# An attention layer's products in column tiles in a projection bank, and the next scores ahead of the transposes

## The reference

```python
q = heads(hidden_states @ W_q)                       # 20 heads of 8
k_t, v_t = heads(text_ehs @ W_k), heads(text_ehs @ W_v)
probs_t = softmax(q k_t^T * attn_scale)              # 128 x 73 for a head
text_out = probs_t @ v_t
qsem = l2norm(probs_t @ text_ehs)                    # 128 x 256 for a head
sem = qsem @ l2norm(ip_ehs)^T                        # 128 x 4
probs_ip = softmax(q k_ip^T * attn_scale + 0.5 * sem) * spatial_mask
out = (text_out + probs_ip @ v_ip) @ W_out + b_out + residual
```

## Time and profile before

| | |
|---|---|
| median of 3 runs | 3484.98 us (3480.99 to 3485.95) |
| profiled execution | 3485.28 us, span 3483.4 us |
| TensorE granted clock, mean | 0.99 |
| busy PE, DVE, ACT, POOL | 96%, 70%, 66%, 38% |
| DMA | 313.84 MB, mean 90 GB/s |

### The profile page before, as it was taken

How to read it: one execution, slowest core, us unless ns; L and a number is a source line. 1 busy time by engine, 2 the same in 40 slices (tenths; PEclk the granted TensorE clock), 3 DMA queues, 4 the chain that set the end, 5 groups by cost and what they waited for, 6 DMA issues and landing times. The chain is left out here.

```text
span 3483.4 us, 96098 instructions
## 1 busy us (share of the span) xinstructions
PE 3335.4 (96%) x34878; PEld 3131.8 (90%) x34878; DVE 2438.3 (70%) x7677; ACT 2314.2 (66%) x6485; POOL 1329.5 (38%) x1657
## 2 busy tenths in 40 slices
PE   5899999999999999999999999999999999999997
PEld 4789999999899999999999899998999999899987
DVE  6657677767767767677767767767677776777655
ACT  4566676766767676676766767676676766767654
POOL 2223343333434433343433434433343333434333
PEclk9999999999999999999999999999999999999998
DMA  6432324223142332324223142332324223142310
GB/s 157 157 116 69 105 63 126 74 86 103 54 123 70 108 90 68 108 63 122 78 83 105 54 123 68 106 94 63 113 64 118 82 82 106 54 124 68 94 51 11
DMA packets 210732, 313.84 MB, mean 90 GB/s; under 512 B 31232, under 2 KB 167520, under 8 KB 210272
## 3 DMA queue, kind: packets, MB, share of 16 engines
q1 hardware_dynamic: 209984, 307.53, 30.5%
q10 hardware_dynamic: 288, 0.16, 0.0%
HBM read 267.97 MB, written 14.42 MB: 81 GB/s over the span
## 5 line engine op out<-in xcount | busy, mean ns | idle before, releaser
L997 ACT ACTIVATE SE<-PS,mx 128x77 f32<-128x77 f32 (+1 forms) x2560 | 674.8, 355 | 271.9 <-DVE mx L1248 271.2
L1461 POOL TENSOR_TENSOR SE<-SE,rs 128x512 f32<-128x512 f32 (+1 forms) x640 | 552.7, 869 | 625.7 <-DVE rs L1270 625.7
L1454 POOL TENSOR_TENSOR n<-qq,p_half 128x4 f32<-128x4 f32 x320 | 327.4, 1023 | 987.0 <-DVE qq L1299 987.0
L1265 DVE TENSOR_REDUCE sums<-SE 128x4 f32<-128x512 f32 (+1 forms) x640 | 368.3, 576 | 217.8 <-ACT SE L997 217.3
L985 ACT ACTIVATE PTs<-PT 128x1024 f32<-128x1024 f32 (+1 forms) x320 | 326.5, 1020 | 242.3 <-PE PT L811 240.7
L933 ACT ACTIVATE qk<-PG 128x512 f32<-128x512 f32 (+1 forms) x640 | 326.3, 510 | 127.2 <-PE PG L612 125.5
L773 PE MATMUL PW<-w_o,OTs 128*128 128x160 f32 x2560 | 408.8, 303 | 0.0
L1248 DVE TENSOR_REDUCE mx<-PS 128x8 f32<-128x1024 f32 (+1 forms) x320 | 323.0, 1010 | 115.6 <-PE PS L793 113.4
L827 PE MATMUL PV<-PTs,v_sb 128*64 128x128 f32 (+1 forms) x5120 | 351.1, 279 | 12.3 <-DVE SE L1291 12.0
L773 PEld LDWEIGHTS PW<-w_o,OTs 128*128 128x128 f32 x2560 | 359.7, 191 | 0.0
L876 PE MATMUL PV<-later 73*128 73x86 f32 x2560 | 331.0, 272 | 2.3 <-ACT later L1006 1.4
(11 more groups left out here) (209 smaller groups left out, 8439.1 us busy)
## 6 DMA issues: line engine op xcount, KB each, us to landing
q_slice<-q_split SPq DMA_DIRECT2D x630, 192.0 KB, 2.4
vc_slice<-vc_split SPq DMA_DIRECT2D x155, 512.0 KB, 4.0
kc_slice<-kc_split SPq DMA_DIRECT2D x150, 256.0 KB, 2.9
q1st<-q_hi SPq DMA_DIRECT2D x320, 32.0 KB, 2.1
k1st<-k_hi SPq DMA_DIRECT2D x160, 38.5 KB, 2.2
xres<-in_x_dram SPq DMA_DIRECT2D x32, 160.0 KB, 2.7
q1st<-q_lo SPq DMA_DIRECT2D x160, 32.0 KB, 2.1
out_dram<-x SPq DMA_DIRECT2D x64, 80.0 KB, 1.6
```

Source lines behind the costliest of these rows:

```text
L997: last = a_(SE[:, n % 4, J * i:J * i + J], PS[:, e, J * at:J * at + J], ACT.Exp, bias=mx[:, q % 2, 4 * e + at:4 * e + at + 1])
L1265: v.tensor_reduce(sums[:, n % 2, :], SE[:, n % 4, 0:4 * J].rearrange("p (i j) -> p i j", j=J), AX, ALU.add)\
L1454: gp.tensor_tensor(n20[:, b % 2, 4 * w:4 * w + 4], qq[:, b % 2, 4 * w:4 * w + 4], p_half[:, 0:4], ALU.pow)\
L1461: gp.tensor_tensor(e, e, rs[:, n % 2, :].unsqueeze(2).to_broadcast([128, 4, J]), ALU.mult)\
```

## The change

1. `probs_v1`'s product becomes a job: it is the first job of slot 0 of the beat after the one it was in, takes a PG bank instead of PV, and stands directly behind `probs_v`. Each of the four matmuls becomes two, with 64 weight columns each, to partitions 0 to 63 and 64 to 127 of the bank (column tiles).
2. `unit_out` moves along, to slot 0 behind `softmax_in`; `unit_norms` and `norms_of` move from slot 0 to slot 1. `tail_slot` grows by one and the tail's jobs shrink by one, so that jobs keep their slots and the VectorE parts are one slot later.
3. At the head of a beat `scores` of the next duo comes before `probs_transposed`.
4. Units of the last group (`alone`) have their scores in turn in PS and PT's second bank, ahead of the transposes of the unit before.

Semaphore `pv1_done` goes; `job_full` stands for it. `probs_v` no longer waits for `on_done`.

```diff
@@ -69,7 +69,7 @@
...
 CTX1_SLOT = {0: 65, 1: 80, 2: 95, 3: 110}
-TAIL_JOB = {"ipT": 7, "ip": 10, "oT1": 13, "y": 16}
+TAIL_JOB = {"ipT": 6, "ip": 9, "oT1": 12, "y": 15}
@@ -349,7 +349,13 @@
...
 def tail_slot(g, b):
-    return 3 * l1_beat(g, W1 * b + W1 - 1) + 7
+    return 3 * l1_beat(g, W1 * b + W1 - 1) + 8
+
+def alone(g, k):
+    return l1_beat(g, k) > DUOS * GROUPS + 1
+
+def scores1_bank(g, k):
+    return PS[:, 0, :] if alone(g, k) and k % 2 else PT[:, 1, :]
...
 def slots(at):
@@ -402,10 +408,12 @@
...
 def jobs_at(t):
...
+    unit = l1_at(t // 3 - 2) if t % 3 == 0 else None
+    products1 = [("pv1",) + unit] if unit else []
...
     first, v = first[:1], v + first[1:]
-    return first + v, [x for x in late_at(t) if x[0] != "v"]
+    return products1 + first + v, [x for x in late_at(t) if x[0] != "v"]
@@ -460,7 +468,7 @@
...
             "down": "down_added", "q1": "q1_done", "k1": "k1_done", "vip": "vip_done",
-            "ctx1": "gv_done", "ipT": "ipT_done", "ip": "o1_done", "oT1": "o1T_done", "y": "y_done"}
+            "ctx1": "gv_done", "pv1": "on_done", "ipT": "ipT_done", "ip": "o1_done", "oT1": "o1T_done", "y": "y_done"}
...
 def bank(name):
@@ -483,7 +491,7 @@
 def wait_gv_used(engine, g, b):
...
     if g0 >= 0:
-        engine.wait_ge(S["pv1_done"], l1_count(g0, W1 * b0 + W1 - 1))
+        engine.wait_ge(S["job_full"], JOB[("pv1", g0, W1 * b0 + W1 - 1)] + 1)
...
 def _(sp):
@@ -818,8 +826,6 @@
...
             pe.wait_ge(S["ots_done"], q)
-        if product1[0]:
-            pe.wait_ge(S["on_done"], product1[0])
@@ -829,7 +835,7 @@
...
-    scored1, turned1, product1 = [0], [0], [0]
+    scored1, turned1 = [0], [0]
...
     def scores1(g, k, turned):
@@ -837,12 +843,15 @@
...
             pe.wait_ge(S["pts_done"], turned)
-        if j > 1:
+        if alone(g, k - 1):
+            pe.wait_ge(S["exp1_done"], j - 2)
+            pe.wait_ge(S["exp_done"], NL0 * GROUPS)
+        elif j > 1:
...
         pe.wait_ge(S["kbd_done"], j)
-        mm(PT[:, 1, 0:4 * T], q1st[:, h, w, 128 * (b % HB):128 * (b % HB) + 128],
+        mm(scores1_bank(g, k)[:, 0:4 * T], q1st[:, h, w, 128 * (b % HB):128 * (b % HB) + 128],
@@ -860,44 +869,47 @@
...
-    def probs_v1(g, k, multiplied):
-
+    def probs_v1(g, k):
+
+        name = ("pv1", g, k)
         b, w, j = k // W1, k % W1, l1_count(g, k)
+        pe.wait_ge(*read_out(JOBS[JOB[name] - len(PG)]))
         pe.wait_ge(S["pts1_done"], j)
-        if multiplied:
-            pe.wait_ge(S["ots_done"], multiplied)
-        if j > 1:
-            pe.wait_ge(S["on_done"], j - 1)
...
             off = D1 * (i % 2)
-            last = mm(PV[:, GV * i + off:GV * i + off + GS + D1], PTs1[0:TT, 128 * i:128 * i + 128],
-                      gv[:, b % 2, 2 * w + i // 2, off:off + GS + D1], start=True, stop=True)
-        last.then_inc(S["pv1_done"], 1)
-        product1[0] = j
+            for c in range(2):
+                last = mm(bank(name)[64 * c:64 * c + 64, GV * i + off:GV * i + off + GS + D1],
+                          PTs1[0:TT, 128 * i + 64 * c:128 * i + 64 * c + 64],
+                          gv[:, b % 2, 2 * w + i // 2, off:off + GS + D1], start=True, stop=True)
+        last.then_inc(S["job_full"], 1)
...
         beat, part = divmod(t, 3)
-        turned, multiplied = min(max(beat + 1, 0), DUOS * GROUPS), min(max(beat, 0), DUOS * GROUPS)
+        turned = min(max(beat + 1, 0), DUOS * GROUPS)
         if part == 0:
+            if duo_at(beat + 1):
+                scores(*duo_at(beat + 1))
...
                 probs_transposed(*duo_at(beat))
-            if duo_at(beat + 1):
-                scores(*duo_at(beat + 1))
...
                 probs_v(*duo_at(beat - 1))
+            if l1_at(beat - 2):
+                probs_v1(*l1_at(beat - 2))
+        ahead = part == 1 and l1_at(beat) and alone(*l1_at(beat))
+        if ahead:
+            scores1(*l1_at(beat), turned)
...
             probs_transposed1(*l1_at(beat - 1), turned)
-        if part == 1 and l1_at(beat):
+        if part == 1 and l1_at(beat) and not ahead:
...
         for name in jobs_at(t)[0]:
-            job(name)
+            if name[0] != "pv1":
+                job(name)
...
             keep_busy(6)
-        if part == 2 and l1_at(beat - 1):
-            probs_v1(*l1_at(beat - 1), multiplied)
@@ -1002,7 +1014,7 @@
...
         if j > 1:
-            act.wait_ge(S["pv1_done"], j - 1)
+            act.wait_ge(S["job_full"], JOB[("pv1",) + divmod(j - 2, GB * W1)] + 1)
...
     def exp1(g, k):
@@ -1012,7 +1024,7 @@
...
         for i in range(4):
-            last = a_(SE1[:, j % 2, TT * i:TT * i + TT], PT[:, 1, T * i:T * i + TT], ACT.Exp,
+            last = a_(SE1[:, j % 2, TT * i:TT * i + TT], scores1_bank(g, k)[:, T * i:T * i + TT], ACT.Exp,
@@ -1253,7 +1265,7 @@
...
         dve.wait_ge(S["s1_done"], j)
-        sc = PT[:, 1, 0:4 * T].rearrange("p (i j) -> p i j", j=T)
+        sc = scores1_bank(g, k)[:, 0:4 * T].rearrange("p (i j) -> p i j", j=T)
@@ -1272,15 +1284,15 @@
     def unit_out(g, n):
...
         j = l1_count(g, n)
-        dve.wait_ge(S["pv1_done"], j)
+        ps = take(("pv1", g, n))
         b, w = n // W1, n % W1
-        o = PV[:, 0:4 * GV].rearrange("p (i d) -> p i d", d=GV)
+        o = ps[:, 0:4 * GV].rearrange("p (i d) -> p i d", d=GV)
...
         for h in range(2):
-            pv = PV[:, 0:4 * GV].rearrange("p (q d) -> p q d", d=2 * GV)\
+            pv = ps[:, 0:4 * GV].rearrange("p (q d) -> p q d", d=2 * GV)\
@@ -1370,7 +1382,7 @@
...
         if sub == 0 and l1_at(beat - 2):
-            unit_norms(*l1_at(beat - 2))
+            unit_out(*l1_at(beat - 2))
@@ -1385,6 +1397,8 @@
...
             prob_sums(g, 2 * d)
+        if sub == 1 and l1_at(beat - 2):
+            unit_norms(*l1_at(beat - 2))
@@ -1399,8 +1413,6 @@
...
                 job(name)
-        if sub == 2 and l1_at(beat - 1):
-            unit_out(*l1_at(beat - 1))
@@ -1495,7 +1507,7 @@
...
             gp.tensor_tensor(cst[:, 1, :], cst[:, 0, :], p_half[0:TS, 0:HB], ALU.pow).then_inc(S["c_pow"], 1)
-        if sub == 0 and l1_at(beat - 2):
+        if sub == 1 and l1_at(beat - 2):
```

More of the change, by code:

```diff
@@ L313, in _ @@
                                      pattern=[[-NIP, GB], [0, H], [-1, NIP]], channel_multiplier=1))
-        names = ["s1_done", "mx1_done", "exp1_done", "pt1_done", "pts1_done", "pv1_done", "x_in0", "x_in1", "x_in2", "c_in", "out_done0", "out_done1", "job_full",
+        names = ["s1_done", "mx1_done", "exp1_done", "pt1_done", "pts1_done", "x_in0", "x_in1", "x_in2", "c_in", "out_done0", "out_done1", "job_full",
                  "ln_stats", "ln_t", "rstd_done", "nx_done", "nT_act", "nT_dve", "bias_added",
```

## The result

The changed kernel takes 3596.89 us (median of 4 runs, 3594.65 to 3598.38) against 3485.17 for the kernel before beside it (4 runs, 3480.99 to 3485.95): a ratio of 1.0323, interval 1.0305 to 1.034. The forecast was 3464, the range ended at 3520, so it was wrong in size and in sign. "The ring binds everywhere", the rival that waits turn up behind the output projection, had the place right and 79 us too little; it named ScalarE's qk reading as the cause, which is the smaller part there.

A forecast was written before the change was run, and what follows sets the result against it. The prediction took PE time and PE's waits to bound the main stage (PE busy 96% of the span). Its terms, -78 - 25 + 41 + 47 - 6 = -21 us, took 3485 to 3464 us; 8-in-10 range 3395 to 3520.

The forecast's parts named there:

- The ring binds everywhere: Rival: in most long beats the job after the output projection waits for ScalarE's qk reading; +54 us, 3518; chance 0.14.
- Step 1: The product in column tiles takes 0.60 us, 0.26 less per unit, in 300 main-stage units: -78 us.
- Serial loads: Rival: the two column tiles load weights in turn, so the tiles give +6 instead of -78; centre 3530, chance 0.10.
- Step 2: PE's waits for GpSimd ahead of the transposes and for VectorE on bank PV go: -25 us.
- Step 3: Ring of two banks: key jobs in five cross beats wait 0.55 us for VectorE's unit_out reading: +41 us.
- Step 4: Cover at a beat's end goes: turns wait for qk and v banks, +47 us; without a turn, output projection covers.
- Step 5: The rest: reordered VectorE and GpSimd steps 0; in the last 128 us a quarter of PE's idle goes, -6 us.

The follow-up runs named there:

- e3: The changed kernel with the product again as four whole matmuls of 128 weight columns, in its new place in the ring: 3691.87 us, 1.0593.
- f2: The changed kernel with VectorE reading v ahead of the second row sums in the first ten beats of a group: 3582.97 us, 1.0286.
- j2: f4 with f2's edit (VectorE reads v before the second sums), without beat 4: 3465.07 us, 0.9946.
- f1: The changed kernel plus a one-column exponential ahead of ScalarE's copy of the transposes after feed-forward jobs, so the table loads earlier: 3567.48 us, 1.0239.
- i4: The changed kernel with the edits of f1, f2 (without beat 4), i2 and i3 together: 3530.63 us, 1.0135.
- i1: The changed kernel with ScalarE reading the second qk job ahead of the second exponential in a group's first ten beats: 3736.89 us, 1.0727.
- i2: The changed kernel with the output projection ahead of the turn on PE, in all beats with a turn: 3580.69 us, 1.0278.
- i3: The changed kernel with the first key job behind the second layer's transposes and scores, on PE alone, in beats 8 to 12: 3606.72 us, 1.0351.
- f3: The changed kernel with the key job of slot 0 moved to slot 1 on all engines, ahead of the other key job: 3589.31 us, 1.0301.
- e4: The changed kernel with the transposes again ahead of the next scores: 3605.73 us, 1.0345.
- e2: The kernel before with only the product in two column tiles, in bank PV at its old place: 3490.26 us, 1.0014.
- e1: The kernel before with only the next scores ahead of the transposes at a beat's head: 3501.71 us, 1.005.
- f4: The kernel before with the next scores first and the early one-column exponential that moves the table load: 3467.88 us, 0.9948.
- j1: The kernel before with only the early one-column exponential that moves the table load ahead of ScalarE's copy: 3483.49 us, 1.0004.

## Why the prediction was wrong, by its steps

**Step 1** held: -5.4 us a group, 81 us, where it said 78; e3 gives 95 with the change of tile form that whole products bring there. A pair takes the 0.075 us that the step took, so 8 pairs are the 0.60; the 0.70 from start to start includes the change of form behind them, which the first layer's product no longer has. "Serial loads" is refuted by the pairs' 0.075 and by e3.

**Step 2** was about right: -1.5 us a group, 22 us, for 25. GpSimd's wait came twice a group, both times in beat 4; now it comes once, in beat 5. The step's "all 12.7 go" missed that.

**Step 3** was right in place and size. In a cross beat of after, the last of the product's reading and the key job that waits for it:

```profile
1006.06 0.45 DVE L1303 TENSOR_TENSOR SE<-PG,SE 128x292 f32<-128x292 f32 x1
...
1006.57 0.90 PEld L634 LDWEIGHTS PG<-cT,kc_slice 128*128 128x128 f32 x6 [0.56 <-DVE SE L1303]
1006.57 1.16 PE L634 MATMUL PG<-cT,kc_slice 128*128 128x312 f32 x6 [0.36 <-DVE SE L1303]
```

0.56 against 0.55 predicted, 75 times, 42 us. From the first load of the qk job to that of the key job it is 0.64 us more than before (1.10 and 0.46), which is the 3.2 us a group of the table. The idle time that counts is that of the weight load; the matmul's 0.36 leaves out the tail that the stall lays open. That is why the list, which reads the matmuls, shows less than the stall costs.

**Step 4 is the one that failed**, in its sentence that in beats without a turn the output projection (more than 1 us) is the cover, priced 0. Those beats cost 5.7 us a group, 86 us, in nine beats. The step followed one reader, ScalarE on the second qk job. The jobs behind the output projection need the v bank as well, and that is 3.4 of the 5.7 us: VectorE reads it in order behind sums that wait for the second exponential, two engines' chains in series, ending where the old product's 0.86 us had been the slack. f2 shows it for the self-attention beats (1, 3 and 8 gain up to 0.79 us when only this order changes), and j2 shows that the same order costs nothing with the product in its old place. For the cross beats 15, 16 and 19 (1.5 us of the 3.4) the trace names the same bank, and no run changed their order. Its turns were undersized too: 5.3 us a group, 80 us for 47, the price of 0.65 being 0.75, 0.74 and 1.1 in the three long beats, 1.17 in the first key beat (of which 0.4 is the second qk job's wait for the keys) and 0.5 in the beat of slot 44, priced 0.1. Part of both is the table load, which no step had: f1 takes 29 us.

**Step 5** had the sign of its last stage wrong: from beat 18 of the last group to the end the kernel after takes 149.2 us instead of 138.5, 11 more where the step took 6 off. Its last 134 us have 33 us of PE idle, where the last 128 of before had 25, at a granted clock of 0.83 and 0.86. Most of the extra time, 9 us, lies within the first ten of the last 22 units. Why is open: no run had item 4 of the change alone, and i4, which has it as well, takes 141.1 us there. A start that is 7 us shorter, up to the head of group 1, which no step had, hides most of it.

Counted as 15 equal groups, the forecast's miss of 133 us is then: 86 in the beats without a turn, 33 at turns, 7 at key jobs, 3 in step 2, 6 in step 5, less 3 in step 1: 132. That step 5 stands here with 6 and not 17 rests on ends that cancel by luck: the start's 7 us, and a group 1 that lost 5 us and not 7.

The remedies confirm the kind of cause but don't undo it. Moving any one wait moves it to the next reader (i1, i2, i3, f3); together they give 66 of 112. What is left in i4 is 142 us of waits, the longest for nT and for the keys. That the product's new place is at the root is shown by e4 against e2 and e3 against e1. That within it the ring of two banks is what binds is argued from the waits; a kernel with a third bank was not tried.

The best version is f4 with or without f2's edit: scores first and the early table load in the kernel before, 0.9948 and 0.9946. That is 16 and 18 us faster than before beside it.

## What to carry to other kernels

Work that stands between a job and the next user of its bank is slack for the readers, and taking it away can cost as much as its own time where the readers are chained (here 0.88 us of wait at the turn in beats 2 and 5, where 0.86 of cover went). Before moving it, follow every bank of the ring to the end of its read-out, on each engine in its order, and not only the bank that the next job asks for. After a reorder that makes an engine idle at one place and late at another, look for what it does once in a while in between (here a table load) and put it into the idle time. And when a version with no more waits than another is slower, compare the granted clock of the same beat in both.

## What the runs showed of the hardware

- Two 64-column tiles of the same rows don't load their weights in turn: pairs of 73x64 weights and 86 moving columns follow every 0.074 us, the two loads of a pair 0.007 us apart, each record 134 to 138 ns long (after); whole 73x128 loads follow every 0.111 us (e3).
- A change of tile form behind the first layer's product costs 0.10 us from matmul start to matmul start (1.02 against 0.92). In the old place, two changes ate the whole gain of the tiles (e2, 1.0014): by its beats, 0.04 us longer where 8 pairs of 0.075 save 0.26, some 0.15 each (an estimate from these).
- A table load of 1.28 us in a beat of 8 to 14 us costs nothing (j1) or 29 us in all (f1), by its place alone.
- The granted clock can fall in the middle of a full stretch: in i3 to 1.2 GHz for 3.4 us in beat 8 of 7 groups of 13, behind 1.4 and 0.85 us of idle PE; in i1 for 6.8 us in most groups, with a wait of 3.2 us in that beat. With 0.83 and 0.85 us of idle in the same places (after) it does not.
